# In the last two heads of an attention stage, VectorE takes a share of the subtraction that GpSimd does alone

## The reference

```python
def _L0_xattn_ref(x, latents, ln_m_g, ln_m_b, ln_l_g, ln_l_b, Wq, Wkv, Wout):
    heads, dim_head = (16, 64)
    scale = dim_head ** (-0.5)
    x = layer_norm(x, ln_m_g, ln_m_b)
    lat = layer_norm(latents, ln_l_g, ln_l_b)
    q = lat @ Wq
    kv = jnp.concatenate([x, lat], axis=1) @ Wkv
    k, v = jnp.split(kv, 2, axis=-1)
    q, k, v = (split_heads(q), split_heads(k), split_heads(v))
    dots = jnp.einsum('bhid,bhjd->bhij', q, k) * scale
    attn = jax.nn.softmax(dots, axis=-1)
    out = jnp.einsum('bhij,bhjd->bhid', attn, v)
    return out.transpose(0, 2, 1, 3).reshape(b, m, heads * dim_head) @ Wout
```

## Time and profile before

| | |
|---|---|
| median of 3 runs | 2348.37 us (2347.03 to 2366.35) |
| the profiled execution | 2350.78 us, its span 2349.0 us |
| mean granted clock of PE over the span | 0.985 |
| busy share of the span | PE 95%, POOL 79%, DVE 79%, ACT 72% |
| attention over all heads | about 120 to 1998 us of the span |
| heads 14 and 15 | about 1773.7 to 1997.7 us |

### The profile page before, as it was taken

How to read it: one execution, slowest core, us unless ns; L and a number is a source line. 1 busy time by engine, 2 the same in 40 slices (tenths; PEclk the granted TensorE clock), 3 DMA queues, 4 the chain that set the end, 5 groups by cost and what they waited for, 6 DMA issues and landing times. The chain is left out here.

```text
span 2349.0 us, 68519 instructions
## 1 busy us (share of the span) xinstructions
PE 2236.9 (95%) x27967; PEld 1468.8 (63%) x27967; DVE 1845.9 (79%) x2969; ACT 1685.8 (72%) x3060; POOL 1858.8 (79%) x1156
## 2 busy tenths in 40 slices
PE   2899999999999999999999999999999998779996
PEld 1356666666666666666666666666666665558884
DVE  8888888888888888888888888888887862448864
ACT  4677777777777777777777777777777776246663
POOL 1789999999999999999999999999999999140001
PEclk9999999999999999999999999999999999789998
DMA  2431314132413241324132413241323000430000
GB/s 92 124 84 42 99 64 125 42 95 68 125 42 95 69 120 46 95 68 120 47 95 68 120 44 97 68 120 43 99 67 95 2 2 2 140 79 2 2 2 13
DMA packets 124634, 165.68 MB, mean 71 GB/s; under 512 B 26392, under 2 KB 100192, under 8 KB 123872
## 3 DMA queue, kind: packets, MB, share of 16 engines
q1 hardware_dynamic: 122176, 157.53, 23.7%
q10 hardware_dynamic: 2144, 3.77, 0.5%
HBM read 99.28 MB, written 61.97 MB: 69 GB/s over the span
## 5 line engine op out<-in xcount | busy, mean ns | idle before, releaser
L682 POOL TENSOR_TENSOR att_prob_low<-att_prob 128x1024 f16<-128x1024 f32 x928 | 1731.4, 1894 | 116.0 <-ACT att_prob L959 57.7
L959 ACT ACTIVATE att_prob<-all_banks 128x512 f32<-128x512 f32 x1888 | 1070.8, 591 | 331.0 <-PE all_banks L768 222.8
L1065 DVE TENSOR_REDUCE att_part<-all_banks 128x2 f32<-128x1024 f32 x581 | 696.3, 1217 | 107.8 <-PE all_banks L728 107.6
L788 PE MATMUL all_banks<-att_v,att_prob 128*128 128x129 f16 x5664 | 583.8, 220 | 0.5 <-ACT att_prob L959 0.3
L788 PEld LDWEIGHTS all_banks<-att_v,att_prob 128*128 128x128 bf16 x5664 | 416.1, 98 | 229.2 <-issue 4.1
L1069 DVE TENSOR_REDUCE att_part<-all_banks 128x1 f32<-128x512 f32 (+1 forms) x686 | 407.5, 638 | 115.6 <-PE all_banks L728 113.6
L802 PEld LDWEIGHTS all_banks<-att_v,att_prob_low 128*128 128x128 f16 x7552 | 327.9, 98 | 127.8 <-POOL att_prob_low L682 7.7
L749 PE MATMUL all_banks<-att_qc,att_kc 128*128 128x512 f16 x1056 | 401.2, 380 | 0.0
L750 PE MATMUL all_banks<-att_qd,att_kd 128*128 128x512 f16 x1056 | 401.0, 380 | 0.0
L802 PE MATMUL all_banks<-att_v,att_prob_low 128*128 128x65 f16 x7552 | 382.6, 194 | 5.5 <-POOL att_prob_low L682 5.1
L792 PE MATMUL all_banks<-att_v,att_prob 128*128 128x64 f16 x1888 | 371.2, 197 | 0.0
(11 more groups left out here) (313 smaller groups left out, 3064.0 us busy)
## 6 DMA issues: line engine op xcount, KB each, us to landing
v_all<-att_stage_v SPq DMA_DIRECT2D x98, 258.0 KB, 2.5
att_kc<-k_high SPq DMA_DIRECT2D x90, 232.0 KB, 3.9
att_v<-v_all SPq DMA_DIRECT2D x28, 483.8 KB
att_v<-v_all SPq DMA_DIRECT2D x28, 451.5 KB
k_high<-att_stage_h SPq DMA_DIRECT2D x98, 128.0 KB, 1.8
k_low<-att_stage_l SPq DMA_DIRECT2D x98, 128.0 KB, 1.9
att_kd<-k_low SPq DMA_DIRECT2D x45, 232.0 KB, 4.2
att_kc<-k_high SPq DMA_DIRECT2D x30, 232.5 KB, 4.4
```

The lines of the kernel that those rows point to most:

```text
L682: pool.tensor_tensor(prob_low[g % NL][:, 0:w], p[:, 0:w], p.bitcast(BF16)[:, 1:2 * w:2], op=ALU.subtract).then_inc(low_split, 1)
L788: pe.matmul(O[:, q, :], w, v[:, e, t, :], start=first, stop=False, skip_group_check=True)
L959: act.activation(prob[g % NP][:, i * BANK:(i + 1) * BANK], S[n % 3], ACT.Exp, scale=SCALE)\
L1065: dve.tensor_reduce(parts[:, n:n + 2], pers.banks[:, 4 + 2 * pair:6 + 2 * pair, :], axis=AX.X, op=ALU.max)\
```

## The change

`dve_columns` gives DVE more. In heads 14 and 15 DVE splits the last 192 columns (`PIECE`) of each odd full unit, and POOL the first 832. In head 15 from unit 24 on (`2 * OFFSET`), where DVE has no maxima left, DVE splits odd full units whole. That is 28 pieces of 192 columns in head 14 and 12 in head 15, and 16 whole units in head 15 (25, 27, and the odd ones from 31 to 57). Even units stay with POOL, the tail units with DVE. In DVE's program the split now stands behind the seed for the next period instead of ahead of it. Every line behind the edits has a number higher by 3 in the changed kernel (L682 becomes L685, L1077 becomes L1080, L1090 becomes L1093).

```diff
@@ -382,6 +382,7 @@
         NORM_AT = 5
+        PIECE = 192
         PERIODS, OFFSET = UNITS // 2, 12
@@ -468,7 +469,9 @@
         def dve_columns(b, g):
 
-            return width(g) if g % SIDE == PAIRS else 0
+            if g % SIDE == PAIRS or b == HEADS - 1 and g % 2 and g >= 2 * OFFSET:
+                return width(g)
+            return PIECE if b >= HEADS - 2 and g % 2 else 0
@@ -1106,11 +1109,11 @@
                     if n is not None:
                         split_task(i + 1, n)
-                    if dve_columns(b, 2 * w + 1):
-                        split_columns(b, 2 * w + 1)
                     u = seeds_before(*next_period(b, w))
                     if u is not None and (w + 1 < PERIODS or with_max):
                         seed(place(b, 2 * w + 1) + len(tiles(2 * w + 1)) + 2, u)
+                    if dve_columns(b, 2 * w + 1):
+                        split_columns(b, 2 * w + 1)
```

## The result

The changed kernel takes 2334.95 us (median of 12 runs, 2330.27 to 2337.29), the kernel before 2349.47 (12 runs). The ratio is 0.992, with a 95% interval of 0.9899 to 0.9942: 0.8% faster. Forecast were 2336 us and a chance of 0.83 for "within 1%".

What follows compares the result with a forecast made beforehand. POOL was taken to set the last half alone and to tie with PE in head 14. Gains of 3.0, 3.0 and 7.0 make 13 us, so 2336 us on the median's scale, range 2328 to 2359.

Steps and rivals of the forecast that it cites:

- head 14: Both halves of head 14: POOL relieved by DVE's pieces, 1.5 us gained a half, 3.0 in all (0 to 5.8).
- head 15, first half: Twelve periods with pieces gain 1.2 us, three without a window 1.8; together 3.0 (1.8 to 4.1).
- second half: Head 15's last half: POOL drops out, PE is next, 48.9 us instead of 55.9, a gain of 7.0.
- POOL's 54.5 ends last: Head 14: POOL's half of 54.5 us outlasts PE's 52.5 to 54, so a half gains 1.5 us.
- DVE's hold on POOL: Pieces in head 14: each takes 0.20 us from POOL (between 0.10 and 0.44), 2.8 us a half.
- I cost it at nothing: Head 14: a piece waiting out a POOL split (up to 1.5 us) costs nothing; PE's window is asked for later.
- The seed ahead of the split costs nothing either: DVE's new order: costs nothing, since PE's `low_pair` waits for the seed and the split is asked for a period later.
- the edges for which I added 0.4 + 1.8: Head 15, second half: 0.4 us for the start and 1.8 for the end, added to PE's 15 x 3.1.
- The slower one: Rival at the 40 pieces: DVE is held out by POOL and becomes the bound, 14 us slower, 2363; chance 0.2.
- The reason given against it: Head 14: DVE asks before POOL's next split is queued, so nothing should be queued behind the odd split.
- PE is the bound in head 14 already: Rival: only the windowless part of head 15 gains, some 7 to 8 us, 2341; chance 0.15.
- The full relief: Rival: POOL's relief is worth its full amount in heads 14 and 15, 19.3 us, 2329; chance 0.15.

Runs made afterwards that it cites:

- e1: Changed kernel without the 192-column pieces, only the 16 whole units of head 15 on DVE: ratio 0.9936 to the kernel before.
- e4: Changed kernel with the low parts of the 40 pieces left out, split by no engine: head 14's halves 53.64 and 53.86 us.
- e10: Changed kernel without DVE's pieces, the last 512 columns of units that POOL splits in heads 14 and 15 left out: head 14's halves 53.64 and 53.86 us.
- e8: Changed kernel without the three pieces in periods where DVE also finishes the maxima of half a head: ratio 0.9932 to the kernel before.
- e3: Changed kernel with DVE's split ahead of its seed again, as in the kernel before: ratio 1.0004 to the kernel before.
- e5: Changed kernel with DVE splitting 512 columns instead of 1024 of odd full units behind unit 24 of head 15: last half 50.51 us.
- e9: Changed kernel with DVE splitting only 16 columns of odd full units behind unit 24 of head 15: last half 55.60 us.
- e11: Kernel before with a small DVE memset directly ahead of head 15's two tail splits: four halves 224.0 us, those splits 3.20 and 3.50.
- e12: Kernel before, unchanged, profiled a second time: four halves 224.0 us, head 15's two tail splits 3.23 and 3.50.
- e6: Changed kernel with pieces of 96 columns instead of 192: ratio 0.9949 to the kernel before.

## Why the prediction was right, and where it was not

The forecast came out because its largest term stands on the right reading: POOL alone set the last half, and no other engine is near behind it there (e1: 47.80 once POOL is relieved). Point by point, forecast and measured gain in us: head 14, 3.0 and 3.2 (112.0 to 108.8); head 15, first half, 3.0 and 3.7; second half, 7.0 and 8.1. The sum, 13 and 15.1. The medians differ by 14.5. The sum is 2.1 us short of the measured 15.1, most of it in head 15.

- **"POOL's 54.5 ends last"** (head 14) was wrong in its reason, and near in its number by luck. PE's own half is 53.64 and 53.86 us (e4, e10), and POOL ends before it at pieces of 192 columns. DVE's hold on POOL was 0.10 us a piece, not 0.20: POOL's 832 columns took 1653 ns on average in the changed kernel and 1575 in e4, without pieces, and its 31 full splits 1919 and 1896: 28 x 0.078 + 31 x 0.023 = 2.9 us for 28 pieces, 0.10 each. With 0.10 the prediction's own sum gives 53.1 us for POOL, below PE's time. POOL is busy for 52.1 us of each half and idle for 2.1 and 2.5, mostly waiting for ACT's exponentials. What the 54.2 and 54.6 have over PE's time comes from one held piece in each half (e8).
- **"I cost it at nothing"** (a piece that waits out the rest of a POOL split) holds for 37 of the 40 pieces (e8's halves are 0.2 us over e4's in all). Where a piece waits out a whole POOL split, behind L1084, the time to the next piece grows by 1 us, and the halves by 1.3 us in all (e8).
- **"The seed ahead of the split costs nothing either"** is true as it stands and misses the point. I priced the reordering at zero and said that seed and split wait for the same exponential. The split also waits for `apply_low` and for POOL's running split. Had the order stayed, the change would have made the kernel's halves 6.4 us longer than before (e3). The order is worth 21.5 us, more than any term of my sum. The text had the pieces of this: it listed what stands behind a held split in the new order (the next takes, a window, the next seed), but never worked out what the old order would have cost, in which this period's seed stands directly behind it.
- **The second half of head 15**: PE's period is 3.20 us, not 3.1, but the edges for which I added 0.4 + 1.8 cost nothing net: 15 x 3.20 = 48.0 is already over the 47.8 measured. That the period of the tail unit has a key tile less fits this, but no run takes the edges apart. ACT's last wait did fall, from 4.04 to 2.00.
- **The rivals.** The slower one (DVE held out past one POOL split) is refuted for the pieces: none of the 40 took over 1.75 us, and e5 and e9 show the same for 512 and 16 columns (2.14 and 1.87 at most). The reason given against it was wrong, though: POOL's next split did stand ready behind the running one, for 36 of 40 pieces, and DVE went in all the same. "PE is the bound in head 14 already" was half right: PE is the next bound, 2.3 us below. The full relief (2329) was not reached: e8's halves gain 16.4 us against its 19.3, and PE's own time in head 14 is what stops it.
- **The rule of the Trainium skill** ("SBUF — State Buffer", "Who interferes with whom"), that the one who issues first holds the interface and the other waits for that instruction, was weighed against two rows and set back. It fits every split of DVE in the changed kernel, e5 and e9 that asked while a POOL split ran; at two splits of the kernel before, and at the same two in e11 and e12, it doesn't, nor at the 18.98 us of e6. The trace that I preferred was right about its own two cases, and wrong as a rule for the 40 others.

## What to carry to other kernels

When work is moved to an engine whose program others wait on, look first at what stands behind it in that engine's order, and at every semaphore that it waits for, the one that frees its output buffer too; put the instruction that others wait for ahead of the one that may be held. The size of the share hardly mattered here (96 to 320 columns, 0.2 us), its place was worth 21.5. And once the limiting engine is relieved, the next one's own time is found by a run that leaves the moved work out, and a second that leaves out more (here e4 and e10, alike to 0.01 us in head 14), which says when to stop.

## What the runs showed of the hardware

- Subtractions of both engines in the same stretch cost POOL little: a piece of 192 columns on DVE was let in between two POOL splits without a gap and cost POOL about 0.10 us. DVE pays with the rest of the running split: its pieces took 0.35 to 1.75 us. I had 0.20 and feared 3.2.
- Who goes first is not one simple rule: two DVE splits of the kernel before are overtaken by POOL in every profile (3.2 and 3.5 us, three profiles), and in the changed kernels none of 287 that POOL's next split followed without a gap. One DVE instruction of the expert layer took 18.98 us beside a busy POOL in e6, and 0.68 to 1.76 in the thirteen other profiles. The cause is open.
- Halves of the attention repeat to 0.02 us between runs, the rest of the program varies between 346.7 and 354.4 us (367.2 once, with the 18.98 us above). Most of the metric's variation comes from there.
